# VectorE takes the first tile's high rows and the low parts of v's last three groups; one projection of q changes its bank

## What is computed

```python
q = x @ Wq.T + bq
k = x @ Wk.T + bk
v = x @ Wv.T + bv
scores = q @ k.T / sqrt(128)
scores = where(adj > 0, scores, -9e15)
att = softmax(scores, axis=-1) @ v
x = layernorm(x + elu(att), axis=-1)
```

## Time and profile before

| what | value |
|---|---|
| median of 3 runs | 428.9 us (428.68 to 429.06) |
| profiled execution, its own time | 429.13 us |
| span in the profile | 427.3 us |
| PE busy | 416.2 us, 97% of the span |
| DVE busy | 360.8 us, 84% |
| ACT busy | 353.8 us, 83% |
| POOL busy | 354.0 us, 83% |
| granted TensorE clock, mean | 0.998 of full speed |

### The profile page before, as it was taken

How to read it: one execution, slowest core, us unless ns; L and a number is a source line. 1 busy time by engine, 2 the same in 40 slices (tenths; PEclk the granted TensorE clock), 3 DMA queues, 4 the chain that set the end, 5 groups by cost and what they waited for, 6 DMA issues and landing times.

```text
span 427.3 us, 11462 instructions
## 1 busy us (share of the span) xinstructions
PE 416.2 (97%) x3470; PEld 311.3 (73%) x3470; DVE 360.8 (84%) x677; ACT 353.8 (83%) x742; POOL 354.0 (83%) x644
## 2 busy tenths in 40 slices
PE   7997999999999999999999999999999999999994
PEld 6764777767777777777777777777777777777784
DVE  3889988888888898888888988888889888888784
ACT  4987788888888889888888898888888988888892
POOL 0596578988898889888988898889888988898875
PEclk9999999999999999999999999999999999999999
DMA  8944999899999999999999999999999999998550
GB/s 253 399 161 111 266 275 251 208 294 263 286 268 254 275 264 267 238 280 266 259 251 280 268 265 244 272 271 263 245 277 271 256 250 271 263 267 225 104 103 21
DMA packets 149794, 104.77 MB, mean 245 GB/s; under 512 B 132755, under 2 KB 141461, under 8 KB 141717
## 3 DMA queue, kind: packets, MB, share of 16 engines
q1 hardware_dynamic: 149344, 104.41, 92.0%
q10 hardware_dynamic: 436, 0.20, 0.2%
HBM read 69.47 MB, written 2.10 MB: 167 GB/s over the span
## 4 chain that ended last, share of the span: by engine, by line
POOL 58%; issue 18%; PE 10%; DMA 4%; ACT 3%; DVE 2%; POOLq 2%; SPq 2%; ACTq 0%; DVEq 0%
POOL p_rows L409 26%; POOL res L423 5%; POOL var_eps L445 4%; POOL rstd L447 4%; POOL att_sum L416 3%; POOL y L428 3%; POOL neg_mean L434 3%; POOL att L418 3%; POOL centred L436 2%; POOL expm L425 2%; DMA p_turned<-p_rows 2%; PE ps_out L967 2%; POOL y_out L451 2%; DMA x_rows<-in_x_dram 2%; POOL var L443 1%
## 5 line engine op out<-in xcount | busy, mean ns | idle before, releaser
L409 POOL TENSOR_TENSOR p_rows<-scores,p_rows 128x256 f16<-128x256 f32 x252 | 177.0, 733 | 7.3 <-ACT p_rows L566 7.1
L696 DVE CUSTOM_DVE_ANT_0 scores<-ps_scores,adj 128x1024 f32<-128x1024 f32 x128 | 155.9, 1218 | 13.0 <-issue 9.3
L549 ACT ACTIVATE scores<-scores,neg_max 128x1024 f32<-128x1024 f32 x128 | 145.8, 1139 | 3.5 <-DVE neg_max L706 3.5
L712 DVE TENSOR_TENSOR p_lo<-ps_t,p_hi 128x512 f16<-128x512 f32 x124 | 82.6, 686 | 28.4 <-ACT p_hi L558 28.3
L682 DVE TENSOR_SCALAR adj<-adj 128x1024 f32<-128x1024 int32 x128 | 103.5, 810 | 0.2
L928 PE MATMUL ps_scores<-k_hi,q_hi 128*128 128x512 f16 x256 | 97.0, 379 | 0.5 <-DVE max_parts L696 0.5
L929 PE MATMUL ps_scores<-k_lo,q_hi 128*128 128x512 f16 x256 | 97.0, 379 | 0.0
L930 PE MATMUL ps_scores<-k_hi,q_lo 128*128 128x512 f16 x256 | 97.0, 379 | 0.0
L967 PE MATMUL ps_out<-v_parts,p_turned 128*128 128x256 f16 x496 | 95.0, 273 | 0.4 <-DMA p_turned<-p_rows 0.3
L967 PE MATMUL ps_out<-v_parts,p_hi 128*128 128x256 f16 x496 | 95.1, 273 | 0.0
L969 PE MATMUL ps_out<-v_parts,p_lo 128*128 128x128 f16 x496 | 88.5, 219 | 0.0
(11 more groups left out here) (121 smaller groups left out, 479.8 us busy)
## 6 DMA issues: line engine op xcount, KB each, us to landing
adj<-in_adj_dram SPq DMA_DIRECT2D x63, 1024.0 KB, 5.3
out_dram<-y_out SPq DMA_DIRECT2D x32, 64.0 KB, 4.9
x_rows<-in_x_dram SPq DMA_DIRECT2D x4, 256.0 KB, 4.4
x_rows<-in_x_dram SPq DMA_DIRECT2D x2, 512.0 KB, 7.6
adj<-in_adj_dram SPq DMA_DIRECT2D x2, 512.0 KB, 7.4
p_turned<-p_rows SPq DMA_TRANSPOSE x63, 4.5
w_rows<-in_L_gnn_Wq_dram ACTq DMA_DIRECT2D x1, 64.0 KB, 2.7
w_rows<-in_L_gnn_Wk_dram ACTq DMA_DIRECT2D x1, 64.0 KB, 3.3
```

What stands on the lines that cost most here:

```text
L409: last = nc.gpsimd.tensor_tensor(p_rows[c][:, w:][:, cols], s_sb[s][:, c * PIECE:c * PIECE + w][:, cols], p_rows[c][:, 0:w][:, cols], ALU. ...
L549: nc.scalar.activation(s_sb[s][:, cols], s_sb[s][:, cols], ACT.Exp, bias=neg_max[:, s:s + 1], accum_out=p_sums[:, s, c:c + 1]).then_inc(ex ...
L696: nc.vector.tensor_tensor_reduce(out=s_sb[s][:, cols], in0=ps_scores[c % 2][:, :], in1=mask_sb[s][:, cols], scale=SCALE, scalar=-3.0e38, o ...
L712: nc.vector.tensor_tensor(p_lo[:, k, :], ps_t[bank_of(s, g)][:, :], p_hi[:, k, :], ALU.subtract).then_inc(plo_ready, 1)
```

## The change

For v's groups 8 to 10 (`V_POOL = 8`) ACT makes only the high half, and DVE makes the low half and the row constant straight from PSUM (`low_of_v`), which signals `v_late`; that also frees the bank. Tile 0's two high copies move from ACT to DVE (`first_high_rows`). q's group 6 is projected into ps_out1 and group 7 into ps_out0, so ps_t0's last user is group 4. `hold_rows(1)` moves from step 6 of period 1 to step 2 of period 2, and `row_logs(1)` behind period 2's row pieces on POOL.

```diff
-Q_BANK = (None, 1, 0, 1, 0, 1, 0, 3)
+Q_BANK = (None, 1, 0, 1, 0, 1, 3, 2)
+V_POOL = 8
+        def wait_v_free(engine, g):
+            if g < V_POOL:
+                engine.wait_ge(v_copied, 2 * g + 2)
+            else:
+                engine.wait_ge(v_late, g - V_POOL + 1)
...
-            for g in range(V_GROUPS):
+            for g in range(V_POOL):
...
             period(1, 1, has_end=False)
+            period(2, 0, has_end=False)
             row_logs(1)
-            period(2, 0, has_end=False)
...
-                nc.scalar.activation(v_full(g), ps_v(g), ACT.Copy).then_inc(v_copied, 1)
+                if g < V_POOL:
+                    nc.scalar.activation(v_full(g), ps_v(g), ACT.Copy).then_inc(v_copied, 1)
...
-                    if j == (1 if not warm and p == 1 else 2) and has_1:
-                        high_rows(p - 1, 1 - n, 0, not warm and p == 1)
-                    if j == (3 if not warm and p == 1 else 6) and has_1:
-                        high_rows(p - 1, 1 - n, 1, not warm and p == 1)
+                    if j == 2 and has_2:
+                        high_rows(p - 1, 1 - n, 0)
+                    if j == 6 and has_2:
+                        high_rows(p - 1, 1 - n, 1)
...
+            def first_high_rows(c):
+                w = DMA_COLS[c]
+                dve.wait_ge(exp_done, c + 1)
+                nc.vector.tensor_copy(p_rows[c][:, 0:w], s_sb[0][:, c * PIECE:c * PIECE + w]).then_inc(rows_hi, 1)
+            def low_of_v(g):
+                tiles = slice(v_tiles(g)[0], v_tiles(g)[-1] + 1)
+                dve.wait_ge(v_copied, V_POOL + g + 1)
+                nc.vector.tensor_tensor(v_parts[:, tiles, 0:D], ps_v(g)[:, :, 0:D], v_parts[:, tiles, D:2 * D], ALU.subtract)
+                nc.vector.tensor_scalar(row_free[:, tiles], ps_v(g)[:, :, D:D + 1].rearrange("p b a -> p (b a)"),
+                                        row_b[:, 0:1], None, ALU.add).then_inc(v_late, 1)
...
+                    if not warm and p == 1 and j in (0, 2):
+                        first_high_rows(j // 2)
                     if not warm:
+                        for g in v_at(STEPS * p + j):
+                            if g >= V_POOL:
+                                low_of_v(g)
                         for m in q_at(STEPS * p + j):
                             low_of_q(m)
...
-            period(1, 1, has_2=False, warm=False, rows_at={6: 1})
-            period(2, 0)
+            period(1, 1, has_2=False, warm=False)
+            period(2, 0, rows_at={2: 1})
...
-                    pe.wait_ge(v_copied, 2 * V_GROUPS)
+                    wait_v_free(pe, V_GROUPS - 1 if Q_BANK[g] == 2 + (V_GROUPS - 1) % 2 else V_GROUPS - 2)
...
-                    pe.wait_ge(v_copied, 2 * g - 2)
+                    wait_v_free(pe, g - 2)
...
                 if first:
-                    pe.wait_ge(v_copied, 2 * V_GROUPS)
-                    pe.wait_ge(v_lo, V_GROUPS)
+                    pe.wait_ge(v_copied, V_POOL + V_GROUPS)
+                    pe.wait_ge(v_lo, V_POOL)
+                    pe.wait_ge(v_late, V_GROUPS - V_POOL)
+                    pe.wait_ge(proj_lo, STEPS)
```

More of the change, by code:

```diff
@@ L136, in attention_kernel @@
         ident_set = sem("ident_set")
+        v_late = sem("v_late")
         wide_set = sem("wide_set")
@@ L558, in high_part, with high_rows @@
                 nc.scalar.activation(p_hi[:, k, :], ps_t[bank_of(s, g)][:, :], ACT.Copy).then_inc(phi_ready, 1)
-            def high_rows(i, s, c, first):
+            def high_rows(i, s, c):
                 w = DMA_COLS[c]
                 act.wait_ge(exp_done, exp_count(i, c))
-                if not first:
-                    act.wait_ge(turned[c], 16 * i)
+                act.wait_ge(turned[c], 16 * i)
                 nc.scalar.activation(p_rows[c][:, 0:w], s_sb[s][:, c * PIECE:c * PIECE + w], ACT.Copy).then_inc(rows_hi, 1)
@@ L636, in _ @@
             attention(LAST - 2, 1)
-            high_rows(LAST, 1, 0, False)
+            high_rows(LAST, 1, 0)
             exp_piece(LAST, 1, 1, False)
@@ L665, in hold_rows @@
                 tiles = slice(*ROW_GROUPS[n])
-                dve.wait_ge(row_added, 1 if n == 0 else V_GROUPS)
+                dve.wait_ge(row_added, 1 if n == 0 else V_POOL)
+                if n == 1:
+                    dve.wait_ge(v_late, V_GROUPS - V_POOL)
                 nc.vector.tensor_scalar(row_neg[:, tiles], row_free[:, tiles], ROW_MOST, -ROW_MOST, ALU.min,
@@ L1025, in _ @@
             period(2, 0, first=True)
-            pe.wait_ge(proj_lo, STEPS)
             period(3, 1)
```

## The result

| | before | with the change |
|---|---|---|
| first measurement, median | 428.79 us (6 runs) | 430.38 us (429.92 to 431.4, 6 runs) |
| ratio, 95% interval | | 1.0042 (1.0031 to 1.0054) |
| once more, median | 428.45 us (29 runs) | 429.43 us (429.04 to 431.23, 12 runs) |
| ratio, 95% interval | | 1.0025 (1.0013 to 1.0038) |
| profiled execution, its span | 429.13, 427.3 us | 429.92, 428.1 us |

The change makes the kernel slower by 1.0 to 1.6 us. The predicted time was 429.5 us, in a range of 428.1 to 431.0. By the first measurement the class it held likeliest, within 0.2%, did not come out: slower did, to which it gave 0.40. The second, with an interval from 0.13 to 0.38%, does not tell the two classes apart.

A forecast was written before the change was run, and what follows sets the result against it. PE was taken as the bound, delayed by DVE's list in period 1: +1.0 us there and -0.45 us for late landings made +0.55, so 429.7 against the profiled execution and 429.5 us against the median, range 428.1 to 431.0.

The forecast's parts named there:

- The bound and DVE's list: Period 1: PE bounds the kernel, waiting for DVE, whose list is the path with 1.44 us of slack.
- The walk: DVE's start times from 28.63 us on: p_lo at 40.3, tile 0's group 6 turned at 41.15, +1.0 us.
- The costs: DVE's added work in period 1: two high copies 1.20 us together, v's low parts with row constants 1.55 us.
- PE's new waits: PE in period 1: v's group 10 until about 30.2, q's group 6 until about 33.5, inside DVE's 1.0 us.
- The clamp at nothing: The clamp, 0.09 us, moved to period 2 ahead of tile 0's last low part, was costed at nothing.
- The masked piece has some slack: Period 2 on DVE: the reason given for costing the moved clamp at nothing.
- The late landings: PE's 0.90 us lost between 78 and 92 us on late transposed rows: bounds 0 and -0.90, middle -0.45 us taken.
- the landings recur whole: Late landings between 78 and 92 us stay in full, giving 429.9, or 431.0 with dear copies; rival's chance 0.30.
- Landings come in time, faster: Rival: DVE meets POOL little, walk +0.3, and the late 0.90 us go whole: -0.6, 428.3 us; chance 0.20.
- It only changes places: Rival: PE's waits for q's and v's banks trade, meetings and landings cancel added work: 428.9 us; chance 0.05.
- the first rival: DVE's copies dear, 1.14 us of spacing each: p_lo at 41.4, 430.6 us, or landings recurring whole; chance 0.30.
- the plain case: Likeliest DVE costs, but late landings between 78 and 92 us recur whole: 429.9 us; counted in a rival's 0.30.

The follow-up runs named there:

- bank_only: Kernel before with only q's sixth and seventh projections in the banks of the change; 428.65 us, ratio 1.0004.
- hold_later: Changed kernel with the clamp (hold_rows) at step 6 of period 2 in place of step 2; 429.28 us, ratio 1.0020.
- q_lo_twice: Kernel before with q's low parts 6 and 7 each made once more on DVE into a spare tile; 429.55 us, ratio 1.0023.
- before_again: Kernel before, unchanged, run once more for a second trace; its profiled execution took 428.85 us.
- act_order: Kernel before with the new q banks and ACT's two high copies placed behind the q_hi that DVE waits for; 428.67 us, ratio 1.0003.
- hybrid: Changed kernel with high copies on ACT at steps 2 and 4, clamp at step 6, only v's last low part on DVE; 427.75 us, ratio 0.9989.
- pool_hold: Changed kernel with v's low parts back on POOL and the clamp at step 6 of period 2; 429.58 us, ratio 1.0034.
- lows_on_pool: Changed kernel with v's low parts all back on POOL, the two high copies staying on DVE; 429.99 us, ratio 1.0046.
- act_order_hold: act_order with the clamp at step 6 of period 2 and row_logs(1) behind POOL's period 2; 428.47 us, ratio 0.9996.
- hybrid_filled: hybrid with two matmuls made twice in two groups of scores to fill PE's idle time; 427.82 us, ratio 0.9996.

## Why the prediction was right or wrong

**The bound and DVE's list: right.** PE's waits decided, and DVE had no slack left. The walk held row by row: with A's start 0.32 us later, it put masked piece 0 at 31.15, the second copy at 33.80, q's low part 5 at 34.83 and p_lo at 40.6; the trace has 31.07, 33.90, 34.96 and 40.76. The +1.0 us at group 6 measured +1.11, and +1.12 in the second trace.

**The costs: right.** The copy took 0.68 where POOL was idle, like the mask, and 1.03 on POOL's group 7, so 0.35 of waiting where 0.38 stood in the walk. v's low parts took 0.55 and 0.41, as by the line through two rows. The row constant took 0.12 to 0.13 to the next start, not 0.09; the masks waited 0.50 and 0.33, not 0.35 each. The Trainium skill, VectorE: DVE Perf Modes, section "The perf-mode tier table", has a copy between float32 operands in SBUF at two elements a cycle, 1227 ns for 2048 elements; 0.69 us for 1024 is an estimate from it. The 0.68 measured agrees, for a copy that writes float16. One cost was left out: the first copy held POOL up as well. POOL's group 7 took 1.48 us (1.04 before), and the low rows began at 30.29 in place of 29.7 plus 0.32.

**PE's new waits: right.** v's group 10 at 30.55 and q's group 6 at 34.04 (30.2 and 33.5, plus 0.32) lie within DVE's delay, and the wait at group 4 went for nothing (bank_only).

**The clamp at nothing: wrong.** "The masked piece has some slack" was taken from no row. The clamp cost 0.34 us, shown by hold_later. The term was mis-sized because the clamp's price was read where POOL was idle, though the prediction itself priced masks that wait for POOL. The Trainium skill, SBUF — State Buffer, section "Who interferes with whom", lists `tensor_scalar` among the operations that can take the shared lock, with the loser blocked entirely; an instruction of 29 columns that waits 0.47 us agrees.

**The late landings: direction right, size and use wrong.** They went whole, not by half: 0.91 and 0.74 in two traces of before, none in three of the change and hold_later. Of the two reasons given, that PE comes later and that tile 0's DMAs go earlier, q_lo_twice speaks against the first; the second is not shown. Against the profiled execution the sum would then be +1.11 +0.34 -0.91 = +0.54, which is the +0.55 predicted: two errors that cancel. With 0.32 for the later start it gives the +0.8 between the two spans. The error behind the wrong class is the step from one execution to the median. The timed runs of before in the second measurement have a median 0.4 us below the 428.85 of before_again and 0.7 below the 429.13 of the profile shown; the five medians of before run from 428.31 to 428.79. So the typical execution seems to lose less in landings than the two profiled ones. With the marks above, and a start of 27.85 (the middle of the traces), some 0.4 us of B are left for a run of 428.45 (an estimate: 428.45 - 1.8 - 276.3 - 109.89 - 12.26 - 27.85 = 0.35). What is not lost can't be won back: 1.11 + 0.34 - 0.35 = 1.1 us, against 1.0 measured there and 1.6 in the first measurement. The estimate hangs on the start, which lies between 27.57 and 28.25 in all traces but one. The remaining 0.5 between the two measurements is not explained. So a time within the range is in part luck: the sum for the profiled execution came out by cancelling errors, and the timed runs lie above it.

**The rivals.** The copies were not dear. The second half of that rival, "the landings recur whole", is close to what the median shows, for another reason: there was less to gain. "Landings come in time, faster" had one half of its condition met, the 0.90 us gone whole, and not the other, a walk of +0.3. "It only changes places" did not happen: group 6 moved by 1.11 us. One figure of the first rival is tied to the wrong case: 0.76 us a copy reaches 429.8 with half the landings gone; with them whole the plain case, at 429.9, is past it already.

## What to carry to other kernels

Work that two edits put on one engine must fit its slack together: each half moved group 6 by at most 0.22 us, both by 1.11. But the mark that moved is not the whole time: with the copies alone group 6 stood where it was, and the timed runs were still 1.0 to 1.7 us slower. A small instruction has no fixed price: 0.17 us where the other engine is idle, 0.64 on top of its work, and the place decides. And a stall that one profiled execution shows must be held against the spread of the timed runs before its removal is booked as a gain.

## What was not expected of the hardware

PE's clock. In three kernels that take waits out of period 1, a part of the executions ran with a lower mean clock: under 0.996 in 4 of 11 of act_order, 2 of 12 of bank_only, 3 of 12 of hybrid, and also in 3 of 11 of q_lo_twice and 4 of 12 of pool_hold; in none of 106 timed runs of before, of 29 of the change and hold_later, of 9 of lows_on_pool, and of 12 each of act_order_hold and hybrid_filled. The trace of bank_only shows where: PE had been idle for 0.81 us ahead of 37.91 and 1.09 us ahead of 39.82, and from 40 to 44 us the grant is 0.60 and 0.55, so mostly the lower of the two levels (1.2 in place of 2.4 GHz). PE in bank_only, a group of scores within the fall and one behind it:

```profile
41.46 0.63 PE L928 MATMUL ps_scores<-k_hi,q_hi 128*128 128x512 f16 x1
41.88 0.63 PE L929 MATMUL ps_scores<-k_lo,q_hi 128*128 128x512 f16 x1
...
43.92 0.38 PE L928 MATMUL ps_scores<-k_hi,q_hi 128*128 128x512 f16 x1
44.13 0.38 PE L929 MATMUL ps_scores<-k_lo,q_hi 128*128 128x512 f16 x1
```

The spacing is 0.42 us in place of 0.21, and from group 6 to group 7 it took 4.75 us in place of 3.08: 1.7 us lost, more than act_order had gained. Before has idle times of 0.75 and 1.10 there and its clock stays at 1.00, so the length of the idle times alone doesn't tell which execution is hit.
